# Residual add of two self attentions: from VectorE to a TensorE product with the identity, and a ScalarE copy

## The reference

```python
x = x + xattn0(layernorm(x), ctx)      # cross attention, 16 heads, 1601 keys a sequence
x = x + attn0(layernorm(x))            # self attention, 16 heads of 16, rotary
x = x + moe(layernorm(x))              # 8 experts, top 2, and a shared one
x = x + mean_mix(layernorm(x), ctx)
x = x + attn1(layernorm(x))            # self attention, 8 heads: 64 wide for q and k, 32 for v; distance bias
x = x + grouped_mlp(layernorm(x))
```

```python
attn = softmax(dots (+ bias), axis=-1)
out  = einsum('bhij,bhjd->bhid', attn, v).transpose(0, 2, 1, 3).reshape(b, n, 256)
return out @ w_out + b_out             # and x + this is the new x
```

## Time and profile before

| | |
|---|---|
| median of three runs | 1295.46 us |
| the three runs | 1291.38 to 1297.83 us |
| the profiled execution | 1299.59 us |
| its span, first to last instruction | 1297.7 us |
| busy in the span | PE 91%, PEld 80%, DVE 53%, ACT 44%, POOL 32% |
| loop of the first self attention | from about 880 to 929 us |
| loop of the second self attention | from about 1192 to 1231 us |

### The profile page before, as it was taken

How to read it: one execution, slowest core, us unless ns; L and a number is a source line. 1 busy time by engine, 2 the same in 40 slices (tenths; PEclk the granted TensorE clock), 3 DMA queues, 4 the chain that set the end, 5 groups by cost and what they waited for, 6 DMA issues and landing times. The chain is left out here.

```text
span 1297.7 us, 32574 instructions
## 1 busy us (share of the span) xinstructions
PE 1174.9 (91%) x13911; PEld 1035.6 (80%) x13911; DVE 693.4 (53%) x1127; ACT 576.8 (44%) x953; POOL 417.7 (32%) x374
## 2 busy tenths in 40 slices
PE   4799999999999999999999999867797999588799
PEld 4789999998999999899999888755575677466588
DVE  6555654754754754754754843345663222555733
ACT  4465555555555555555555555334621223121400
POOL 5632432432432422422422416445153122112000
PEclk9899999999999999999999999977888999789999
DMA  6936746756655755755665653186022211405055
GB/s 201 213 80 157 165 100 151 165 107 147 164 112 142 165 117 138 165 120 135 163 126 134 150 120 78 50 251 226 1 82 74 58 58 41 150 9 215 2 189 189
DMA packets 61255, 165.78 MB, mean 128 GB/s; under 512 B 24840, under 2 KB 35288, under 8 KB 58040
## 3 DMA queue, kind: packets, MB, share of 16 engines
q1 hardware_dynamic: 58088, 157.52, 48.3%
q0 software_dynamic: 1872, 5.13, 1.1%
q10 hardware_dynamic: 1152, 1.05, 0.2%
HBM read 73.24 MB, written 11.05 MB: 65 GB/s over the span
## 5 line engine op out<-in xcount | busy, mean ns | idle before, releaser
L504 DVE TENSOR_REDUCE xa_mx<-xa_sc 128x2 f32<-128x804 f32 x256 | 243.7, 992 | 41.9 <-PE xa_sc L665 41.8
L458 ACT ACTIVATE xa_pt<-xa_sc 128x1024 f32<-128x1024 f32 (+1 forms) x224 | 212.4, 963 | 107.5 <-PE xa_sc L681 107.2
L681 PE MATMUL xa_sc<-xa_queries,xa_keys 104*128 104x128 f32 (+1 forms) x1664 | 221.5, 276 | 0.5
L681 PEld LDWEIGHTS xa_sc<-xa_queries,xa_keys 104*128 104x128 f32 (+1 forms) x1664 | 196.5, 187 | 17.6 <-issue 3.9
L590 PE MATMUL xa_pj<-xa_ctx_hi,xa_wk 128*128 128x400 f32 (+1 forms) x512 | 158.5, 352 | 1.2 <-DVE xa_qst L532 0.9
L590 PE MATMUL xa_pj<-xa_wv,xa_ctx_hi 128*128 128x256 f32 (+1 forms) x832 | 155.1, 285 | 0.1
L665 PE MATMUL xa_sc<-xa_keys,xa_queries 96*128 96x402 f32 x512 | 135.1, 365 | 9.8 <-DMA xa_keys<-xa_kst_hi 6.7
L692 PE MATMUL xa_op<-xa_pt,xa_values 128*32 128x64 f32 x6656 | 135.9, 222 | 8.7 <-ACT xa_pt L458 4.1
L337 POOL TENSOR_TENSOR xa_ctx_lo<-xa_raw,xa_ctx_hi 128x1600 fp32r<-128x1600 f32 (+1 forms) x32 | 115.9, 3624 | 78.0 <-DVE xa_ctx_hi L497 75.3
L342 POOL TENSOR_TENSOR xa_kst_lo<-xa_wk,xa_kst_hi 128x400 fp32r<-128x400 f32 x64 | 67.3, 1052 | 227.3 <-ACT xa_kst_hi L411 227.2
L590 PEld LDWEIGHTS xa_pj<-xa_wv,xa_ctx_hi 128*128 128x128 f32 (+1 forms) x832 | 126.1, 184 | 7.9 <-issue 6.3
(11 more groups left out here) (325 smaller groups left out, 1798.0 us busy)
## 6 DMA issues: line engine op xcount, KB each, us to landing
xa_keys<-xa_kst_hi SPq DMA_DIRECT2D x256, 200.2 KB, 6.1
xa_keys<-xa_kst_lo SPq DMA_DIRECT2D x128, 200.2 KB, 5.3
xa_raw<-in_ctxT SPq DMA_DIRECT2D x15, 1601.0 KB, 9.2
gf_w<-in_gf_w SPq DMA_DIRECT2D x16, 1024.0 KB, 7.2
moe_ex<-in_moe_ex SPq DMA_DIRECT2D x8, 1088.0 KB, 19.0
xa_queries<-xa_qst SPq DMA_DIRECT2D x96, 32.0 KB, 5.3
moe_slots_in<-in_moe_empty SPq DMA_DIRECT2D x1, 2967.0 KB, 25.1
moe_xs<-moe_slots_in SPq DMA_DIRECT2D x23, 129.0 KB, 2.1
```

The costliest lines, as they stand in the source:

```text
L458: nc.scalar.activation(PT[ptslot(step)][0:rows, 0:nt], SC[bank(step)][0:rows, 0:nt], ACT.Exp, scale=float(D0) ** -0.5).then_inc(ex_done, 1)
L504: nc.vector.tensor_reduce(mx[:, u // 2, 2 * (u % 2):2 * (u % 2) + 2], SC[bank(step)][:, :, 0:MXN], AX.X, ALU.max).then_inc(mx_done, 1)
L681: last = mm(SC[bank(step)][0:rows, kk, a * P:(a + 1) * P], KS[:, 2 * a + h, kt * P:kt * P + rows], QS[b % 2][:, 2 * a + h, :], start=True, ...
```

## The change: the sum is made in PSUM

In both attentions `project` gets a third product, the identity with the old tokens `X[:, t]`, accumulated into the same bank `WP`. ScalarE then copies the bank over `X[:, t]` (`added`) behind `exps` in its step. VectorE's addition is gone; it keeps the statistics, which now stand behind `normalise`. The wait for GpSimd's bias moves from VectorE to TensorE.

```diff
@@ tensor: project
                 for k in range(2):
-                    last = mm(WP[:, 0, 0:D], oT[:, k, :], W["o"][:, k, :], start=k == 0, stop=k == 1)
-                last.then_inc(y_full, 1)
+                    mm(WP[:, 0, 0:D], oT[:, k, :], W["o"][:, k, :], start=k == 0, stop=False)
+                if t == 0:
+                    pe.wait_ge(bias_added, T)
+                mm(WP[:, 0, 0:D], c["ident"], X[:, t], start=False, stop=True).then_inc(y_full, 1)
@@ vector
-            def add(t):
-                dve.wait_ge(bias_added, T)
-                dve.wait_ge(y_full, t + 1)
-                xs = X[:, t]
-                nc.vector.tensor_tensor(xs, xs, WP[:, 0, 0:D], ALU.add).then_inc(y_ev, 1)
-
+            def summed(t):
                 dve.wait_ge(y_ev, t + 1)
-                nc.vector.bn_stats(stats[:, t], xs).then_inc(stats_done, 1)
+                nc.vector.bn_stats(stats[:, t], X[:, t]).then_inc(stats_done, 1)
 
             def step(t, j, behind, ahead):
                 if ahead:
                     less_max(t + 1)
+                normalise(t)
                 if behind:
-                    add(t - 1)
-                normalise(t)
-
-            over_tiles(dve, step, lambda: less_max(0), lambda: add(T - 1))
+                    summed(t - 1)
+
+            over_tiles(dve, step, lambda: less_max(0), lambda: summed(T - 1))
@@ scalar
+            def added(t):
+
+                act.wait_ge(y_full, t + 1)
+                nc.scalar.activation(X[:, t], WP[:, 0, 0:D], ACT.Copy).then_inc(y_ev, 1)
@@ scalar: step
                 if ahead:
                     exps(t + 1)
+                if behind:
+                    added(t - 1)
+                if ahead:
                     if t < T - 2:
                         place_values(t + 2, j)
@@ scalar: after the loop
-            over_tiles(act, step, before, lambda: turned_out(T - 1))
+            def last_out():
+                turned_out(T - 1)
+                added(T - 1)
+
+            over_tiles(act, step, before, last_out)
```

## The result

| | before | change |
|---|---|---|
| median of 18 runs each | 1296.09 us | 1300.60 us |
| ratio, 95% interval | | 1.003 [1.002, 1.004] |
| the same comparison, timed again with the experiments | | 1.0016 [1.0000, 1.0032] |
| profiled execution: span | 1297.7 us | 1295.3 us |

What follows compares the result with a forecast made beforehand. The prediction saw the second attention's loop closing through TensorE, ScalarE and VectorE, not VectorE alone. First attention 0.4, second 1.3 and ends 0.8 summed to +2.5 us: 1298.0 us against the median 1295.46, range 1293.2 to 1302.5.

Steps and rivals of the forecast that it cites:

- The forecast's mechanism: Second attention: taking VectorE's addition and statistics off the chain wins 0.25 us a step, the product on TensorE pays back 0.43.
- an unlucky median: Whole kernel: runs differ by 6.5 us, so a median of a few moves by 2 or 3 us for no cause.
- The 0.2 us for the first projection at the lower clock: First attention: the first projection lies where the clock is partly at its lower level, adding 0.2 us.
- The two hundredths on VectorE's side: First attention: the statistics' 0.43 us fit VectorE's idle time ahead of the maximum but for a few hundredths.
- The term of 0.4 us: Sum of the first attention's steps: 0.4 us longer, range 0 to 1.2.
- the row's gap of about 0.3 us ahead of a weighing: Weighing starts 0.31 us after the projection's last record starts, read in the second attention and applied to both.
- ScalarE's hand-over to VectorE: Ends of both attentions: VectorE needs up to 0.1 us to see ScalarE's copy instead of 0.04.
- Rival 1: Second attention: VectorE is the bound, each step gives back the addition's 0.42 us; whole -2.1, 1293.4 us; chance 0.08.
- Rival 2: Clock level shifts in later blocks: gained once 1296.0 us, chance 0.10; lost once +4.5, 1300.0, 0.12; lost twice or more 0.05.
- a level that changes at another place: Changed profile: a clock level changing at another place was listed among the signs that the forecast was wrong.
- Rival 3: Second attention: the product disappears in the loop, step 3.53 to 3.78 us, ends +0.8; whole 1295 us; chance 0.05.

Runs made afterwards that it cites:

- two_products: The change with the product with the identity made twice; ratio 1.0066 against the kernel before, second loop 4.42 us a step, first 5.05.
- no_product: The change without the product with the identity, ScalarE copying the projected output alone; ratio 0.9979 against the kernel before, second loop 3.55 us a step.
- second_only: The change in the second self attention alone, the first as in the kernel before; ratio 1.0000 against the kernel before, second loop 3.99 us a step.
- before_again: The kernel before, unchanged, timed against itself; ratio 0.9997, steps 4.60 us in the first loop and 3.78 in the second.
- first_only: The change in the first self attention alone, the second as in the kernel before; ratio 1.0009 against the kernel before, first loop 4.62 us a step.
- add_behind: The kernel before with only VectorE's addition and statistics moved behind normalise; ratio 0.9972 against the kernel before, timed again 0.9985; second loop 3.56 us a step.

## Why the prediction was right, and where it was off

- **No change that half a per cent can tell, and slightly slower.** Forecast +2.5 us, 1298.0 us, with a range up to 1302.5. Measured 1300.6 us, +4.5 (2.6 to 5.2) and +2.1 (0 to 4.1). The loops and ends in the profiles add up to +2.2: 1.4 (second loop), 0.14 (first loop, 7 x 0.02) and 0.64 (ends). The forecast's mechanism is shown by two_products and no_product. That the first timing also fell inside the range is owed to the room made for rivals and for an unlucky median, not to the sum. Why it gives more than 2.2 is not settled; the loops and ends of the profile don't hold it, and the second timing moved back towards 2.2, more than half of it by a longer kernel before.
- **Second attention.** Forecast 3.96 a step, and 3.53 without the product; measured 3.99 and 3.55. The reciprocal alone takes 0.21 us when it no longer runs into the statistics ahead of it, 0.19 before, and such hundredths are the rest. The product's 0.43 was taken from a neighbouring operation of the same shape, and the doubled product confirms it. Seven steps: +1.3 forecast; +1.41 from the first reciprocal to the last in second_only against before_again, where the clock rose at about the same place.
- **First attention.** The fit in TensorE's idle time was forecast at 0.02 to 0.05 us, measured 0.02. The 0.2 us for the first projection at the lower clock was wrong: in first_only the first step is 6.61 us against 6.57, with the clock low for both. The two hundredths on VectorE's side that I allowed for did not show either. The term of 0.4 us measures 0.15 to 0.2. The rule that the prediction takes from the Trainium skill ("TensorE: Matmul & The Clock Gate", Part 2, weight loads pulled ahead of matmuls in flight) gave 0 for these steps as the prediction used it; the row's gap of about 0.3 us ahead of a weighing was the better guide, and it is there again (the product's second record starts at 1206.79 + 0.59 - 0.38 = 1207.00, the weighing and its first weight load at 1207.32). The page makes a condition that the prediction left out: the row groups must not conflict, or the load must go to the background weight buffer. Which part of that fails at this place no run here shows.
- **The ends.** Forecast +0.4 each, measured +0.31 and +0.33. ScalarE's hand-over to VectorE, for which I allowed up to 0.1 us, took 0.03 (925.65 to 925.68).
- **ScalarE.** Its idle time ahead of `oT` fell from 0.74 to 0.56 us in the first loop and from 0.84 to 0.62 in the second; it never ran out, and no_product shows the copy free.
- **Rival 1** (VectorE is the bound of the second attention) is refuted: without its addition VectorE waits 0.95 us in every step, and the step grew. What it had right shows in add_behind: VectorE's instructions did stand in the loop, but by their order, not by their number.
- **Rival 2** (the clock). The forecast knew that its levels shift by a few us, but not how freely: unchanged code has them at another place in the first loop from one execution to the next. The forecast named a level that changes at another place as a sign of being wrong; the changed profile does show it (the full clock over 890 to 894, where the kernel before had the lower), but so does before_again with no edit at all, so the sign can't tell. The first timing's +4.5 us is the number that this rival gives for one level lost. The comparison at the same clock, 2.3 us, leaves about 0.5 us for it; that an edit here moves the levels for good is not shown and not excluded.
- **Rival 3** is refuted by the product's full price in the second loop.

## What to carry to other kernels

When a wait goes round several engines, ask first whether the instruction on the chain has to be ahead there: moving one line on VectorE (3.78 to 3.55 us a step) did more than moving its work to two other engines (3.99). Here an addition that TensorE took over was nearly free only where TensorE waited (0.02 us a step against 0.44); if it must be made there, put it ahead of the wait and not behind it (3.62 against 3.99 with the same instructions). For edits worth 2 us of 1300, read the step from the profile and take the timed ratio only as a bound on what else may have moved.

## What the runs showed of the hardware that I had not expected

- A copy of 128x256 fp32 out of PSUM takes VectorE 0.41 us, as long as its addition with a second operand from SBUF (0.41 to 0.42), and ScalarE 0.36 to 0.38.
- TensorE's first product after a wait starts a stream badly: in the second loop four records span 1.10 us behind a wait and 1.03 directly behind another product, so filling the wait gave 0.07 us on top.
- The same program had the full clock over 890 to 894, early in the first loop, in one execution and the lower level in another, which alone moved its first step from 4.60 to 6.57 us. The mean granted clock of the 18 runs of the change lies between 0.953 and 0.960; the shortest of them (1297.15 us) has the highest and the longest (1303.14 us) the lowest.
